# A Mamba layer and a Hadamard feed-forward on one core: dense steps by a new table of slots, and the copies of each tile's last states made by ScalarE

## The reference, cut to what matters

```
x = x + L0_attn(layernorm(x))      # inside: h = u + mamba(rmsnorm(u)); h + mlp(rmsnorm(h))
x = x + L0_ffn(layernorm(x))       # inside: fwht(silu(x W1) * (x W3)) W2
```

```
h[t] = exp(dt[t] * A) * h[t-1] + dt[t] * x[t] * B[t]
y[t] = sum over the 32 states of h[t] * C[t]
```

## Time and profile before

| What | Value |
|---|---|
| three runs | 1238.37, 1240.99, 1241.42 us; median 1240.99 |
| the profiled execution's own time | 1238.53 us |
| its span, first to last instruction | 1236.7 us |
| mean granted TensorE clock | 0.935 |
| GpSimd busy | 925.7 us (75%) |
| ScalarE busy | 605.5 us (49%) |

### The profile page before, as it was taken

The page is one execution under the profiler, slowest core; times in us unless marked ns, Lnnn a source line. Parts: engine busy times, 40 slices in busy tenths (PEclk is TensorE's granted clock), DMA queues, the critical chain, the costliest instruction groups (busy, mean ns, idle before and its releaser), DMA issues. The chain is left out here.

```text
span 1236.7 us, 12998 instructions
## 1 busy us (share of the span) xinstructions
PE 1080.3 (87%) x3848; PEld 541.3 (44%) x3848; DVE 1022.8 (83%) x1161; ACT 605.5 (49%) x1092; POOL 925.7 (75%) x564
## 2 busy tenths in 40 slices
PE   2566769999898989999898989999898989898988
PEld 1221224445444454445444554445454544445445
DVE  3378989998898989998899889998999899996222
ACT  3645465545654455545654545545654545443210
POOL 0379998877998788876998788877998799874100
PEclk9676679999999999999999989999999999898889
DMA  5798976774767675774758575674856676550000
GB/s 201 183 248 174 204 174 137 151 165 109 189 137 168 139 180 135 160 164 109 186 126 184 132 175 137 155 167 115 192 132 143 141 187 140 121 109 17 1 0 17
DMA packets 99493, 176.38 MB, mean 143 GB/s; under 512 B 12960, under 2 KB 21600, under 8 KB 98784
## 3 DMA queue, kind: packets, MB, share of 16 engines
q1 hardware_dynamic: 98272, 171.36, 60.7%
q0 software_dynamic: 1152, 4.19, 1.0%
HBM read 150.34 MB, written 8.39 MB: 128 GB/s over the span
## 5 line engine op out<-in xcount | busy, mean ns | idle before, releaser
L959 POOL TENSOR_TENSOR h_s<-h_s,c_s 128x1024 f32<-128x1024 f32 x256 | 604.2, 2362 | 107.6 <-DVE h_s L772 97.6
L546 ACT ACTIVATE p_dt<-p_dt,an_s 128x512 f32<-128x512 f32 x512 | 334.4, 660 | 351.9 <-PE p_dt L408 351.5
L408 PE MATMUL p_dt<-kdt,pick_s 128*128 128x512 f32 x512 | 349.5, 694 | 61.6 <-DVE h_s L772 60.7
L772 DVE TENSOR_TENSOR_SCAN h_s<-p_dt,carry,bt_s 128x512 f32<-128x512 f32 x256 | 321.7, 1273 | 18.2 <-ACT p_dt L546 17.0
L772 DVE TENSOR_TENSOR_SCAN h_s<-p_dt,bt_s 128x512 f32<-128x512 f32 x256 | 305.5, 1213 | 36.5 <-ACT p_dt L546 27.7
L464 PE MATMUL p_r<-nT,w_s 128*128 128x512 f32 x512 | 243.9, 604 | 4.4 <-ACT nT L697 4.4
L939 POOL TENSOR_TENSOR bt_s<-bt_s,b_s 128x1024 f32<-128x1024 f32 x96 | 226.6, 2360 | 19.6 <-DMA bt_s<-dx_rows 19.5
L757 DVE TENSOR_TENSOR bt_s<-bt_s,p_b 128x1024 f32<-128x1024 f32 x160 | 193.1, 1207 | 8.0 <-DMA bt_s<-dx_rows 7.7
L408 PEld LDWEIGHTS p_dt<-kdt,pick_s 128*128 128x128 f32 x512 | 101.5, 202 | 208.8 <-DVE h_s L772 127.4
L453 PE MATMUL p_r<-nT,gu_s 128*128 128x512 f32 x352 | 169.9, 603 | 2.4 <-ACT nT L692 2.4
L419 PE MATMUL p_y<-h_s,ysel_s 128*32 128x512 f32 x1024 | 152.2, 669 | 16.6 <-POOL h_s L959 16.6
(11 more groups left out here) (85 smaller groups left out, 738.6 us busy)
## 6 DMA issues: line engine op xcount, KB each, us to landing
bt_s<-dx_rows SPq DMA_DIRECT2D x512, 256.0 KB, 5.3
kdt<-st_dt SPq DMA_DIRECT2D x64, 128.0 KB, 5.7
tok<-in_x SPq DMA_DIRECT2D x8, 512.0 KB, 7.1
xr_s<-xb_s SPq DMA_DIRECT2D x64, 64.0 KB, 4.0
dx_rows<-dx_s SPq DMA_DIRECT2D x16, 256.0 KB, 5.5
b_s<-xb_s SPq DMA_DIRECT2D x64, 64.0 KB, 5.0
xo<-in_x SPq DMA_DIRECT2D x8, 512.0 KB, 7.3
out<-res POOLq DMA_DIRECT2D x8, 512.0 KB, 6.8
```

What stands on the lines that cost most here:

```text
L408: nc.tensor.matmul(p_dt[DT_BANK[u]][:, :], sel, kdt[:, h, p // 16, :], start=True, stop=True)\
L546: A(p_dt[DT_BANK[u]][:, :], p_dt[DT_BANK[u]][:, :], ACT.Exp, scale=an_s[:, c:c + 1]).then_inc(a_dA, 1)
L772: V.tensor_tensor_scan(h_s[:, u % 8, :], p_dt[DT_BANK[u]][:, :], bt_s[:, u % 16, :], carry[:, u:u + 1] if par else 0.0, ALU.mult, ALU.add) ...
L959: G.tensor_tensor(h_s[:, two, :], h_s[:, two, :], c_s[:, h, :].unsqueeze(1).broadcast_to([P, 2, T]), ALU.mult)\
```

## The change

`place_steps` no longer works slots out. `PLAN` now gives each step its number of instructions and the first and last slot over which they are spread evenly. Order and slots are both new: uT is split around slot 2, xb comes in front of out, dtr behind z, the steps of gate/up and of w1/w3 are no longer one by one in turn, and several slots hold none. The slots with a name of their own move, `YG` and `Y1` being those of `gate_y` (36 and 3 before). `POOL_PAIRS` is written out. The copies of last states leave GpSimd: `keep_carry` makes them on ScalarE, two slots after the pair's first unit, behind that slot's decay, and GpSimd's product with C and the scans of the next tile wait for its semaphore `a_car`. GpSimd's `one_s` of ones goes.

```diff
-POOL_PAIRS = [k for k in range(PAIRS) if k % 8 in (0, 3, 5)]
+POOL_PAIRS = [0, 3, 5, 8, 11, 13, 16, 19, 21, 24, 27, 29]
...
-PLAN = ([("c1", 0, 2, .86)]
-        + [("uT", k, 4, .2) for k in range(2)]
-        + [("dtr", 0, 2, .86)]
-        + [("out", k, 4, .43) for k in range(2)]
-        + [("xb", 0, 2, .86)]
-        + [("z", k, 2, .86) for k in range(2)]
-        + [("hT", k, 4, .2) for k in range(2)]
-        + [s for f in range(GB) for s in (("gate", f, 2, .86), ("up", f, 2, .86))] + [("gate", GB, 2, .86)]
-        + [("dtp0", 0, 1, .86)]
-        + [("down", k, 12, .43) for k in range(2)]
-        + [("c0", 0, 2, .86)]
-        + [("xT", k, 4, .2) for k in range(2)]
-        + [s for f in range(HB) for s in (("w1", f, 2, .86), ("w3", f, 2, .86))]
-        + [("dtp1", 0, 1, .86)]
-        + [("w2", k, 16, .43) for k in range(2)])
+PLAN = [
+    ("c1", 0, 2, 0, 0), ("uT", 0, 4, 1, 2), ("uT", 1, 4, 2, 2), ("xb", 0, 2, 2, 2), ("out", 0, 4, 3, 4),
+    ("out", 1, 4, 4, 5), ("z", 0, 2, 6, 8), ("z", 1, 2, 7, 9), ("dtr", 0, 2, 10, 10), ("hT", 0, 4, 11, 11),
+    ("hT", 1, 4, 11, 11), ("gate", 0, 2, 12, 12), ("gate", 1, 2, 12, 12), ("up", 0, 2, 13, 15),
+    ("gate", 2, 2, 15, 15), ("up", 1, 2, 15, 16), ("gate", 3, 2, 15, 19), ("up", 2, 2, 17, 19),
+    ("up", 3, 2, 19, 19), ("gate", 4, 2, 20, 22), ("up", 4, 2, 21, 22), ("dtp0", 0, 1, 24, 26),
+    ("gate", 5, 2, 24, 24), ("down", 0, 12, 26, 28), ("down", 1, 12, 29, 31), ("c0", 0, 2, 33, 36),
+    ("xT", 0, 4, 36, 36), ("xT", 1, 4, 36, 36), ("w1", 0, 2, 36, 36), ("w1", 1, 2, 37, 39), ("w3", 0, 2, 37, 38),
+    ("w1", 2, 2, 41, 41), ("w3", 1, 2, 41, 41), ("w1", 3, 2, 42, 42), ("w3", 2, 2, 42, 42), ("w3", 3, 2, 43, 45),
+    ("w1", 4, 2, 45, 45), ("w1", 5, 2, 45, 47), ("w3", 4, 2, 48, 48), ("w1", 6, 2, 49, 50), ("w3", 5, 2, 51, 51),
+    ("w3", 6, 2, 51, 51), ("w1", 7, 2, 52, 52), ("dtp1", 0, 1, 53, 54), ("w3", 7, 2, 53, 53),
+    ("w2", 0, 16, 55, 57), ("w2", 1, 16, 60, 61)
+]
...
-X_SLOT = 58
-XL_SLOT = 54
-XO_SLOT = 44
-KEPT_SLOT = 5
-DT_STEP = 8
-SUM_COST = .9
+X_SLOT = 59
+XL_SLOT = 57
+XO_SLOT = 27
+KEPT_SLOT = 8
+DT_STEP = 1
+YG = 35
+Y1 = 2
...
+            s = first + j * (last - first + 1) // n
             slots.setdefault(s, []).append((q, j))
             ends[stage, k] = s
...
+            def keep_carry(i, k):
+
+                act.wait_ge(v_sc, i * U + 2 * k + 2)
+                two = slice(2 * k % 8, 2 * k % 8 + 2)
+                A(carry[:, 2 * k:2 * k + 2], h_s[:, two, T - 1], ACT.Copy).then_inc(a_car, 1)
+
...
                     if (units if u + 1 < U else pre):
                         decay(i + (u + 1) // U, (u + 1) % U)
+                    if units and par == 0 and u % 2 == 0 and u >= 2:
+                        keep_carry(i, u // 2 - 1)
...
+                    if units and par == 0 and u == U - 1:
+                        keep_carry(i, PAIRS - 1)
...
                     if par:
-                        dve.wait_ge(g_car, (i - 1) * (PAIRS // 2) + k + 1)
+                        dve.wait_ge(a_car, (i - 1) * (PAIRS // 2) + k + 1)
...
-                    if post and u == 3:
+                    if post and u == Y1:
                         gate_y(pt, other, 1)
                         gate_z(pt, other, 1)
...
                         if par == 0:
-
-                            G.tensor_tensor(carry[:, u - 1:u + 1], h_s[:, two, T - 1], one_s[:, :], ALU.mult)\
-                                .then_inc(g_car, 1)
-                            pool.wait_ge(g_car, i * (PAIRS // 2) + k + 1)
+                            pool.wait_ge(a_car, i * (PAIRS // 2) + k + 1)
```

More of the change, by code:

```diff
@@ L71 @@
-GAP = 5
-AFTER = {("uT", 0): (None, 1), ("out", 0): (None, 3), ("hT", 0): (("out", 1), GAP), ("down", 0): (("gate", GB), 2),
-         ("c0", 0): (("down", 1), 3), ("xT", 0): (("down", 1), GAP)}
-RING = 3
-FIRST_SLOT, LAST_SLOT = 0, 62
-X_SLOT = 58
-XL_SLOT = 54
-XO_SLOT = 44
-KEPT_SLOT = 5
-DT_STEP = 8
-SUM_COST = .9
[L84 to L96, removed]
+PLAN = [
[5 rows of a table added]
+    ("gate", 5, 2, 24, 24), ("down", 0, 12, 26, 28), ("down", 1, 12, 29, 31), ("c0", 0, 2, 33, 36),
[5 rows of a table added]
+]
@@ L97, in place_steps @@
+RING = 3
+X_SLOT = 59
[5 more added lines that the diff above has]
+Y1 = 2
+def place_steps():
+    slots, ends = {}, {}
+    for q, (stage, k, n, first, last) in enumerate(PLAN):
         for j in range(n):
[L98 to L101, removed]
+            s = first + j * (last - first + 1) // n
             slots.setdefault(s, []).append((q, j))
             ends[stage, k] = s
-            at += c
@@ L105, in place_steps @@
[L105 to L110, removed]
+    return slots, ends
+STEPS, ENDS = place_steps()
 BANK = {step[:2]: q % RING for q, step in enumerate(PLAN)}
@@ L140, in build @@
         half_s = sb("half_s", [P, 8])
-        one_s = sb("one_s", [P, 2])
         kdt = sb("kdt", [P, 2, 2, T], F32R)
@@ L208, in build @@
         v_fa, v_hd, v_o = sem("v_fa"), sem("v_hd"), sem("v_o")
-        g_rr, g_rr2, g_car, g_bt = sem("g_rr"), sem("g_rr2"), sem("g_car"), sem("g_bt")
+        g_rr, g_rr2, g_bt, a_car = sem("g_rr"), sem("g_rr2"), sem("g_bt"), sem("a_car")
         g_hc, g_r, g_r2, g_r3, g_dx, g_hx = (sem(f"g_{n}") for n in ("hc", "r", "r2", "r3", "dx", "hx"))
@@ L423, in dense @@
             def dense(q, j, i, par, on):
-                stage, k, n, _ = PLAN[q]
+                stage, k, n = PLAN[q][:3]
                 t = tile_of(stage, i)
@@ L730, in _ @@
             V.memset(half_s[:, :], -0.5).then_inc(w_zero, 1)
-            V.memset(one_s[:, :], 1.0).then_inc(w_zero, 1)
-            dve.wait_ge(w_zero, 2)
+            dve.wait_ge(w_zero, 1)
             dve.wait_ge(l_w["c"], 80)
@@ L840, in body @@
                                                 st_dt[:, 0, :].bitcast(F32), ALU.subtract).then_inc(v_dtl, 1)
-                    if units and u == 36:
+                    if units and u == YG:
                         gate_y(i, par, 0)
-                    if units and u == 37:
+                    if units and u == YG + 1:
                         gate_z(i, par, 0)
@@ L919, in _ @@
             G = nc.gpsimd
-            pool.wait_ge(w_zero, 2)
+            pool.wait_ge(w_zero, 1)
             def x_norm(t):
```

## The result

The changed kernel takes 1208.32 us (median of four runs, 1206.96 to 1209.06) against 1240.58 for the kernel before, a ratio of 0.9741 with a 95% interval of 0.9725 to 0.9758: faster by 32.3 us, where 34 were forecast. The total is close to the forecast. (Of all executions behind this document one, of e12, was in a slow state: 1423.93 us at a granted clock of 0.735; no ratio counts it.)

What follows compares the result with a forecast made beforehand. VectorE, busy 126.0 of 137.7 us per tile, was taken as the bound, TensorE nearly as loaded at 123.5. Gains of 49.4 us less 11.4 for bursts and 4 for clock gave 1241 - 34 = 1207 us, range 1190 to 1236.

Steps and rivals of the forecast that it cites:

- the signs that the text named: Tiles 1-6 131 to 133 us, VectorE 126; no waits at slots 9, 55, 56; gate_y under 0.5; even/odd gap unchanged.
- Start of the tile: Earlier sum before gate_y at tile borders gains 10.5 us; xb's copy gone from slot 7 gains 7.4 at slot 9.
- Softplus and XL_SLOT: Softplus a slot later, normalisations in slot 57: waits of 25.6 us at slots 55 and 56 leave 2.1, gain 23.5.
- The walk: Timing of ScalarE and VectorE from slot 52 to 56: about 0.3 us of wait stays per tile.
- w1 and w3: Steps rearranged: half the places with 18 to 19 us of tanh waits in tiles 1 to 7 go, gain 8.
- cost of bursts: Slots 41-42 and 50-62: TensorE's work overruns VectorE's by 0.5 and 1.2 us; charged 1.9 x 6 = 11.4.
- Clock: TensorE at quiet slots 39-40 and 58-59: clock partly falls to half rate; charged 0.7 us per tile, 4 in all.
- 2.4 us: Tile 5 against tile 3 in the earlier profile: price of one more half-clock stretch.
- Carry: 128 copies from GpSimd to ScalarE: cost taken as 0, bounds nothing to 26 us; GpSimd's product 0.2 to 0.5 later.
- The rival on ScalarE's queue: Carries' waits hold back tanh and softplus in even tiles; all 26 us show, 1233 us; chance 0.05.
- The prediction's 39 us by the Trainium skill: ScalarE's 128 copies at the skill's budget of about 0.3 us an instruction: an estimated 39 us.
- TensorE taking over: Bank waits in slots 42, 52 and 12, overrun and half clock: 10.4 us per tile, 1254 us; chance 0.10.

Runs made afterwards that it cites:

- e12: Changed kernel with copies back on GpSimd, second half of w2 over slots 58 to 61 and uT whole in slot 1: 1200.68 us, ratio 0.9695.
- e3: Changed kernel with XL_SLOT back to 54 instead of 57 alone: 1220.75 us, ratio 0.9852 to the kernel before.
- e11: Changed kernel with all eight transposes of uT in slot 1, in front of the sum: 1205.58 us, ratio 0.973.
- e9: Changed kernel with xb behind out again in slots 5 and 6, and gate_y in slot 3: 1225.16 us, ratio 0.989.
- e10: Changed kernel with xb alone back behind out, in slots 5 and 6, gate_y staying in slot 2: 1212.70 us, ratio 0.9787.
- e4: Changed kernel with w1 and w3 one step a slot again, in turn, slots 36 to 51: 1214.08 us, ratio 0.9795.
- e6: Changed kernel with slots 0 to 10 of the old table, gate_y in slot 3, KEPT_SLOT 5: 1231.73 us (median of ten runs), ratio 0.9937.
- e1: Changed kernel with the copies of last states back on GpSimd: 1200.23 us, ratio 0.9695.
- e5: Changed kernel with the copies back on GpSimd and idle copies on ScalarE, for which nobody waits: 1203.08 us, ratio 0.9713.

## Why the prediction was right, and where it was not

**Right: what bounds it, and that the stalls could go.** VectorE's work of 126 us per tile stayed, its idle time fell by 21.5 us in six tiles; the time came from there. The parts undone one by one give 23.4 (start of the tile), 12.4 (XL_SLOT) and 5.8 (w1 and w3), together 41.6, and the copies take 8.1: 33.5 net against 32.3 measured. By the ratios it is 24.3 + 13.8 + 6.7 - 5.7 = 39.1 against 32.1, so that they add up is not shown. What is shown is that a wait of VectorE that goes, and comes back nowhere else, is paid in full: its work per tile does not change. From the changed kernel to e3 its waits in tiles 1 to 6 grow by 12.9 and these tiles by 13.1 us.

Of the signs that the text named, VectorE's work (126 us), the scan of slot 9, gate_y and the copies' 0.2 us came as it said. Tiles 1 to 6 were to take 131 to 133 us and took 131.8 to 135.4; the scan of slot 56 still waits 0.5 to 1.7; and even tiles are longer than odd ones, which they were not before. VectorE's idle time per tile is 8.1 us, not far from the 9 at which the text would have called itself wrong.

**Start of the tile: 10.5 + 7.4 = 17.9 forecast, 23.4 measured.** Both waits went as the text had it: gate_y's from 12.3 us at six borders to under 0.2, and that at slot 9. Two details were wrong. uT's split was given a share; e11 shows none. And the earlier gate was seen as a cost that the earlier sum covers; e9 shows it to be worth 12.5 us in the order of e10, since out, and with it all of TensorE's work up to scan 9, hangs on it. What hangs on the gate was named nowhere in the text.

**Softplus and XL_SLOT: 23.5 forecast, about 15.8 by the waits.** The waits behind softplus (slots 55 and 56 before, 56 and 57 now) went from 25.6 to 9.8 us over seven tiles. The walk had 0.3 left per tile; 0.8 is left in tiles without copies and 2.0 in those with. e3 puts 12.4 on XL_SLOT alone. The mechanism was right, the gain a third smaller than forecast.

**w1 and w3: 8 forecast as gain, 11.4 as cost of bursts.** The waits for tanh went almost altogether in the tiles, 18 us over tiles 1 to 7 instead of 8. The cost of the bursts was named for slots 41 and 42 and for 50 to 62 (0.5 and 1.2 per tile; these add to 1.7, where the text charges 1.9). It came in slot 63 of tiles 1 to 6 (9.0) and in slot 40 (5.2 more than before). The term that was put at nothing without a reason is slots 11 to 32, whose order changes as well: 12.1 us more of waits, 5.7 of them without the copies. Taken together, the tanh waits gave 10 more than forecast, and the bursts with slots 11 to 32 cost 8.5 more (19.9 against 11.4). e4 measures w1 and w3 alone at 5.8; within tiles 1 to 6 their waits, 13.1 less 7.2, agree with that.

**Clock: +4 forecast, and it went the other way.** In the stretch from 180 to 1100 us TensorE had the lower level for some 38 us before and 17 after, summed from single microseconds; the mean granted clock rose from 0.935 to 0.948. The step that failed is that an empty slot is a quiet time. (Two readings behind it were loose too: of tiles 1 to 6, tile 4 had no such stretch behind slots 32 to 34, and the one at tile 5's border lasted 6.8 us, twice as long as the others, so 2.4 us is the price of a double one.) After 652.96 in tile 4 of the changed kernel TensorE issued this:

```profile
652.96 0.80 PE L387 MATMUL p_dt<-kdt,pick_s 128*128 128x512 f32 x1
653.69 1.06 PE L398 MATMUL p_y<-h_s,ysel_s 128*32 128x512 f32 x8
654.68 1.98 PE L443 MATMUL p_r<-nT,w_s 128*128 128x512 f32 x4
656.10 1.25 PE L387 MATMUL p_dt<-kdt,pick_s 128*128 128x512 f32 x3
```

Slots 38, 39, 40 and the head of 41: the last line holds three spreads in 1.25 us. TensorE came out of slots 36 to 38 behind what it was allowed to issue (the spread of slot 39 may go once scan 38 has ended, at 652.4, and went at 656.10), and the two empty slots let it catch up; it was at no time idle there, nor in slots 58 and 59. The two stretches that hold slots 39 to 42, and the one behind slots 32 to 34 in tile 3:

```profile
652.00:656.00 4.00, 4.00 (x16) 1.41 (x15) 3.18 (x4) 1.69 (x5) 3.12 (x2) 1.00 0.36 66
656.00:660.00 4.00, 4.00 (x12) 2.08 (x11) 3.38 (x5) 3.04 (x7) 2.15 (x1) 1.00 1.02 227
...
510.50:514.50 4.00, 3.95 (x12) 2.42 (x12) 4.00 (x5) 3.00 (x7) 3.30 (x3) 0.57 0.59 151
```

Full clock in the first two, 0.57 in the last, after slots in which TensorE did stand. In tiles 1 to 6 all stretches at the lower level lie behind slots 32 to 34 (tiles 2 and 3 only); the three at the borders are gone with the waits there. But standing is not enough either. Slots 33 and 34 of tile 3, where the clock fell behind them, and of tile 4, where it did not:

```profile
506.71:510.18 3.47, 1.50 (x9) 0.34 (x9) 3.47 (x5) 2.48 (x7) 2.90 (x3) 1.00 1.08 216
642.11:645.46 3.35, 1.49 (x9) 0.34 (x9) 3.35 (x6) 1.98 (x6) 3.27 (x4) 1.00 1.00 218
```

TensorE is busy 1.5 us in both; what decides between the two isn't shown. The rule of the Trainium skill (TensorE: Matmul & The Clock Gate, "HAM oscillation — how this bites in real kernels") is about idle gaps. The trace agrees as far as every fall between 180 and 1100 us lies behind a stretch in which TensorE stood, and none behind an empty slot in which it did not; tile 4 shows that such a stretch need not bring one. What e6 lost with the clock is estimated above from its ten runs (4 us); what the whole change gained by it isn't separated.

**Carry: 0 forecast, 8.1 lost.** This is the step that failed outright (8.1 by the medians, 5.7 by the ratios). The text said that GpSimd's product starts 0.2 to 0.5 us later; by the medians of e1 and the changed kernel it starts 2.2 later (1.0 and 3.2 us after the scan), and 53 of GpSimd's waits, up to 3.7 us long, end with ScalarE's copy. It held the copy to come as soon as scan u-1 is done, and looked only at what the copy delays on ScalarE (e5: little). It did not ask what ScalarE does in front of the copy: the exponential of u+1 needs a spread that TensorE issues behind its dense steps. Where TensorE is late, a copy whose data are ready stands behind it, and GpSimd with it. The rival on ScalarE's queue had the sign and the mark to look for, tiles with copies longer than the others, but the wrong mechanism, 0.05 as its chance and a price of 26 us three times too high. The prediction's 39 us by the Trainium skill (ScalarE: Activation LUTs, "Rules for kernel authors") goes by a figure that the page gives for an instruction with a bias per partition; these copies have none and took 195 ns, 25 us in all.

**TensorE taking over** did not happen, but its waits did. VectorE's list can't show them; TensorE's weight loads for w1 and w3 do, where they wait for the gate of w1 to free a bank:

```profile
PEld p_r L443 <- DVE th_s L889: 9.0, 18, 0.9
```

In slot 42 of tiles 1 to 7 it is 0.66 to 0.86 us (1.15 in the text), in slot 52 of the odd ones 0.24 (1.65 in the text). So the rival named the right places; its sizes were too large, above all in slot 52, and the 4.8 of half clock per tile that it needed did not come.

That the total came within 2 us of the forecast is in part luck: the tanh waits (10 us) and the start of the tile (5.5) gave more than forecast, and softplus (7.7), the bursts with slots 11 to 32 (8.5) and the copies (8.1 or 5.7) took it back.

## What to carry to other kernels

When a small instruction moves from a busy engine to an idle one, ask what stands in front of it in the new engine's order and what that waits for; the idle engine here was idle because it stood waiting for TensorE, and the consumer inherited the wait. Where one engine's work fills nearly the whole time, as VectorE's does here, find the wait that gates the most work behind it (here gate_y in front of out) and move that one first; then add up all its waits again, since here more than half of what was removed came back in other slots. An empty slot in a table is idle time only if the engine arrives there on time.

## What was not expected of the hardware

The granted clock rose with a burstier table, 0.935 to 0.948: from 180 us on it fell only behind stretches in which TensorE really stood, wherever the table had its empty slots, and not behind all of those. ScalarE's copy of two elements per partition took 195 ns (189 to 227 over 128), about the 191 of GpSimd's: the engine that had more room was no faster at it, and neither figure was what the move cost.
